# Attention token stages: tail keys of four heads on four 64x64 tiles of TensorE, output halves in two banks

## What is computed

```python
q = _split_heads(query @ Wq.T + bq)
k = _split_heads(key @ Wk.T + bk)
v = _split_heads(value @ Wv.T + bv)
scores = jnp.einsum('bhqd,bhkd->bhqk', q, k)
scores = scores * tau[:, :, None, None] + delta[:, None, None, :]
p_attn = jax.nn.softmax(scores / jnp.sqrt(DK), axis=-1)
x = jnp.einsum('bhqk,bhkd->bhqd', p_attn, v)
x = x.transpose(0, 2, 1, 3).reshape(query.shape[0], -1, H * DK)
return x @ Wo.T + bo
```

## Time and profile before

| | |
|---|---|
| runs | 3376.84 us median of 3 (3376.42 to 3385.39) |
| profiled execution | 3380.68 us, its span 3378.9 us |
| mean granted TensorE clock | 0.978 |
| token stage of layer 0, 12 turns in the middle | 199.4 to 831.4 us |
| token stage of layer 1, 12 turns in the middle | 2040.5 to 2648.1 us |

### The profile page before, as it was taken

One profiled execution on the slowest core, in us unless ns is written; L12 is line 12 of the kernel. 1 busy time (PEld: TensorE's weight loads), 2 busy tenths in 40 slices (PEclk: granted clock), 3 DMA queues, 4 the chain that ended last, 5 costly groups with the idle time before them and its releaser, 6 DMA issues. The chain is left out here.

```text
span 3378.9 us, 55655 instructions
## 1 busy us (share of the span) xinstructions
PE 3197.8 (95%) x17324; PEld 2506.5 (74%) x17324; DVE 2735.5 (81%) x5290; ACT 1560.9 (46%) x5449; POOL 2081.7 (62%) x2335
## 2 busy tenths in 40 slices
PE   7999999999979999999999699999999969999998
PEld 5677777777648888888888577777777757778886
DVE  4788888888677887888887379999999879967775
ACT  1766767667521111111111377777777745321111
POOL 1776666766536777777777477777777753443333
PEclk8999999999979999999999899999999989999999
DMA  7345454454465667676766544555554457730111
GB/s 218 100 137 173 122 166 140 137 174 125 141 174 154 171 169 175 170 166 166 176 164 156 112 128 133 160 163 143 151 172 135 138 164 286 274 103 13 26 13 25
DMA packets 284781, 490.97 MB, mean 145 GB/s; under 512 B 54018, under 2 KB 74818, under 8 KB 283778
## 3 DMA queue, kind: packets, MB, share of 16 engines
q1 hardware_dynamic: 243698, 408.87, 39.6%
q0 software_dynamic: 32256, 77.65, 12.4%
q10 hardware_dynamic: 8592, 1.57, 0.3%
HBM read 250.32 MB, written 136.96 MB: 115 GB/s over the span
## 5 line engine op out<-in xcount | busy, mean ns | idle before, releaser
L915 ACT ACTIVATE c_pr<-ps,t_negmax 128x154 f32<-128x154 f32 x1024 | 385.7, 393 | 180.8 <-DVE t_negmax L684 178.6
L684 DVE TENSOR_REDUCE t_negmax<-ps 128x4 f32<-128x616 f32 x512 | 403.6, 788 | 53.3 <-PE ps L980 52.6
L915 ACT ACTIVATE t_pr<-ps,t_negmax 128x154 f32<-128x154 f32 x1024 | 385.6, 393 | 105.8 <-DVE t_negmax L684 101.4
L707 DVE COPY t_pTm<-ps 128x512 f32<-128x512 f32 x448 | 306.0, 683 | 127.3 <-PE ps L993 123.0
L609 POOL TENSOR_TENSOR t_pr<-t_pr,t_inv 128x512 f32<-128x512 f32 x256 | 275.7, 1077 | 191.0 <-DVE t_inv L699 189.3
L609 POOL TENSOR_TENSOR c_pr<-c_pr,t_inv 128x512 f32<-128x512 f32 x256 | 272.0, 1063 | 196.4 <-DVE t_inv L699 195.0
L980 PE MATMUL ps<-t_kst,t_stack 98*128 98x154 f32 x2048 | 353.0, 291 | 26.3 <-DMA t_stack<-t_q_low 10.1
L980 PEld LDWEIGHTS ps<-t_kst,t_stack 98*128 98x128 f32 x2048 | 279.6, 194 | 38.9 <-issue 17.8
L81 PE MATMUL ps<-e_xT_high,e_wgu_high 128*128 128x512 f32 x768 | 302.4, 394 | 1.4 <-DVE e_xT_low L1508 1.4
L83 PE MATMUL ps<-e_xT_high,e_wgu_low 128*128 128x512 f32 x768 | 299.6, 390 | 0.0
L82 PE MATMUL ps<-e_xT_low,e_wgu_high 128*128 128x512 f32 x768 | 299.4, 390 | 0.0
(11 more groups left out here) (373 smaller groups left out, 9320.9 us busy)
## 6 DMA issues: line engine op xcount, KB each, us to landing
t_stack<-t_q_high SPq DMA_DIRECT2D x1016, 64.0 KB, 2.0
c_wgu_in<-in_gate_upT SPq DMA_DIRECT2D x32, 1536.0 KB, 6.4
t_stack<-t_q_low SPq DMA_DIRECT2D x512, 64.0 KB, 2.0
x_dram<-c_wide_rows SPq DMA_DIRECT2D x32, 1024.0 KB, 7.8
c_wd_in<-in_downT SPq DMA_DIRECT2D x32, 768.0 KB, 4.5
t_xbo<-in_x SPq DMA_DIRECT2D x16, 1024.0 KB, 7.0
xw_dram<-t_z SPq DMA_DIRECT2D x16, 1024.0 KB, 5.3
t_xbo<-x_dram SPq DMA_DIRECT2D x16, 1024.0 KB, 11.0
```

Source lines behind the costliest of these rows:

```text
L684: dve.tensor_reduce(negmax[:, u, :], flat[:, at:at + HG * APART].rearrange("p (h n) -> p h n", h=HG)[:, :, 0:KEYS], AX, ALU.max, negate=Tr ...
L707: dve.tensor_copy(pTm[:, g % 2, :, t * P:(t + 1) * P], ps[:, 4, :].rearrange("p (h n) -> p h n", h=HG)).then_inc(s["pTm"], 1)
L915: op = act.activation(pr[:, u % 4, h, :], flat[:, col:col + KEYS], ACT.Exp, bias=negmax[:, u, h:h + 1], accum_out=total[:, u, h:h + 1])
```

## The change

The tail values of two heads become one block of 52 rows (`PROWS`) and 64 columns, and four such products run on four 64x64 tiles of the array: array rows 0 to 51 and 64 to 115 (`HIGH` is 64), columns 0 to 63 and 64 to 127. Each covers 256 tokens. The result lies in two banks, 5 and 6, the first 256 tokens in one and the rest in the other. For the second two token tiles of a group the heads are kept in swapped pairs (`place`), so that their tails come out of the transpose on the other half of the rows. The main products run as eight matmuls of 256 tokens instead of four of 512. Queries and projections move from bank 6 to bank 7.

The four tail transposes of a group run together in a step of their own (`tail_transposes`, steps `TT`), and `p_transposes` has four transposes instead of five. `tails` has eight slots instead of four, and POOL clears it once at the start of the stage. The transposes use bank 5 too, so they wait until the output of the group before is out of it (`oT_out`). The steps of `V`, `PT`, `OO` and `OL` change. In layer 1, `values` of group 2 go from step 3 to step 1 and those of group 3 from 6 to 7; in layer 0, `V` stays.

```diff
-    for h in range(HG):
-        sp.dma_start(scr[f"vt{l}"].rearrange("b (n h) (g e d) -> h (b n) g e d", h=HG, e=HG, d=DK)[h, :, :, h, :],
-                     k["vt"][:].rearrange("n (g e d) -> n g e d", e=HG, d=DK)[:, :, h, :]).then_inc(s["stored"], 16)
+    for b in range(B):
+        for e in range(2):
+            sp.dma_start(scr[f"vt{l}"][b, e * KTAIL:(e + 1) * KTAIL, :].rearrange("n (q e d) -> n q e d", e=2, d=DK)[:, :, e, :],
+                         k["vt"][b * KTAIL:(b + 1) * KTAIL, :].rearrange("n (q e d) -> n q e d", e=2, d=DK)[:, :, e, :]
+                         ).then_inc(s["stored"], 16)
...
-        V = (15, 24, 2, 7) if gate else (15, 23, 3, 6)
+        V = (15, 24, 2, 7) if gate else (15, 23, 1, 7)
+        TT = (12, 20, 30, 5) if gate else (12, 20, 29, 5)
...
-        OL = (23, 30, 4, 9) if gate else (17, 27, 5, 9)
+        OL = (18, 27, 4, 9) if gate else (17, 26, 3, 9)
...
-        PT = (11, 19, 28, 3) if gate else (11, 19, 27, 4)
-        OO = (16, 26, 2, 7) if gate else (15, 24, 4, 7)
+        PT = (12, 20, 30, 5) if gate else (12, 20, 29, 5)
+        OO = (16, 25, 2, 7) if gate else (15, 24, 2, 7)
...
-            sp.dma_start(vt[:, g * P:(g + 1) * P], scr["vt%d" % l][b, :, g * P:(g + 1) * P]).then_inc(s[f"v_in{g}"], 16)
+            for r in (0, HIGH):
+                sp.dma_start(vt[r:r + PROWS, g * P:(g + 1) * P],
+                             scr["vt%d" % l][b, :, g * P:(g + 1) * P]).then_inc(s[f"v_in{g}"], 16)
...
+            pool.memset(tails[:], 0.0).then_inc(s["ready"], 1)
...
+                if v % TG == 0:
+                    reached(pool, s["tail_mm"], GROUPS * i + v // TG - 1)
...
-                dve.tensor_tensor(oT[1][:, k, :], ps[:, B_BANK, :], oT[0][:, k, :].bitcast(F32),
+                dve.tensor_tensor(halves(oT[1][:, k, :]), ps[:, O_BANKS, 0:HALF], halves(oT[0][:, k, :]).bitcast(F32),
                                   ALU.subtract).then_inc(s["oT_out"], 1)
...
             def p_tail_out(i, g):
-                act.wait_ge(s["p_mm"], UNITS * i + TG * (g + 1))
+                act.wait_ge(s["tail_mm"], GROUPS * i + g + 1)
...
                 for h in range(HG):
-                    pe.transpose(ps[:, 4, h * P:(h + 1) * P], pr[:, v % 4, h, 0:P], ident[:])
-                pe.transpose(ps[0:TROWS, 5, t * P:(t + 1) * P], tails[:, v % 4, :],
-                             ident[:]).then_inc(s["p_mm"], 1)
+                    mm = pe.transpose(ps[:, 4, h * P:(h + 1) * P], pr[:, v % 4, place(h, t), 0:P], ident[:])
+                mm.then_inc(s["p_mm"], 1)
+
+            def tail_transposes(i, g):
+
+                pe.wait_ge(s["normed"], 2 * (UNITS * i + TG * g + TG))
+                reached(pe, s["oT_out"], GROUPS * i + g)
+                for t in range(TG):
+                    at = (HIGH + PROWS) * ((TG * g + t) % 8)
+                    mm = pe.transpose(ps[0:HIGH + PROWS, 5, t * P:(t + 1) * P], tails[:, at:at + HIGH + PROWS], ident[:])
+                mm.then_inc(s["tail_mm"], 1)
...
-                pe.matmul(ps[:, B_BANK, :], vt[:, g * P:(g + 1) * P], pTt[:], start=True, stop=False,
-                          skip_group_check=True)
-                for h in range(HG):
-                    mm = pe.matmul(ps[h * DK:(h + 1) * DK, B_BANK, :], vm[:, g * P + h * DK:g * P + (h + 1) * DK],
-                                   pTm[:, g % 2, h, :], start=False, stop=True, skip_group_check=True)
+                for half in range(2):
+                    for q in range(2):
+                        r = HIGH * (q if half == 0 else 1 - q)
+                        pe.matmul(ps[HIGH * q:HIGH * (q + 1), 5 + half, 0:HALF],
+                                  vt[r:r + PROWS, g * P + HIGH * q:g * P + HIGH * (q + 1)],
+                                  pTt[r:r + PROWS, half * HALF:(half + 1) * HALF], start=True, stop=False,
+                                  skip_group_check=True)
+                for half in range(2):
+                    for h in range(HG):
+                        mm = pe.matmul(ps[h * DK:(h + 1) * DK, 5 + half, 0:HALF],
+                                       vm[:, g * P + h * DK:g * P + (h + 1) * DK],
+                                       pTm[:, g % 2, h, half * HALF:(half + 1) * HALF], start=False, stop=True,
+                                       skip_group_check=True)
                 mm.then_inc(s["pv"], 1)
...
+                    if at in TT[:3] and cur:
+                        tail_transposes(i, TT.index(at))
+                    if at == TT[3] and prev:
+                        tail_transposes(i - 1, GROUPS - 1)
                     if at in V[:2] and cur:
                         values(i, V.index(at), batch)
```

More of the change, by code:

```diff
@@ L28 @@
 GROUPS = HEADS // HG
-TROWS = HG * KTAIL
+PROWS, HIGH = 2 * KTAIL, P // 2
 DC = D // P
@@ L46 @@
 UNITS = TG * GROUPS
+HALF = GTOK // 2
 KROWS = 3 * DK + 2
@@ L214, in key_value_phase @@
         dhigh, dlow = (sb(f"delta_{part}", [P, B, KEYS], F32R) for part in ("high", "low"))
-        zero = sb("zero", [TROWS, D])
+        zero = sb("zero", [PROWS, D])
         ps = c["ps"]
@@ L231, in _ @@
                 sp.dma_start(scr[f"vt{l}"].rearrange("b t d -> t b d"),
-                             zero[:].unsqueeze(1).to_broadcast([TROWS, B, D])).then_inc(s["cleared"], 16)
+                             zero[:].unsqueeze(1).to_broadcast([PROWS, B, D])).then_inc(s["cleared"], 16)
             for half in range(2):
@@ L314, in token_phase @@
         pr = c["pr"] if gate else sb("pr", [P, 4, HG, KEYS])
[L315 to L318, removed]
+        tails = sb("tails", [P, 8 * (HIGH + PROWS) + HIGH - PROWS])
+        pTm, pTt = sb("pTm", [P, 2, HG, D]), sb("pTt", [HIGH + PROWS, D])
+        total, mv = sb("total", [P, UNITS, HG]), sb("mv", [P, 2, TG, 2])
         ve, rstd = sb("ve", [P, 2, TG]), sb("rstd", [P, 2, TG])
@@ L407, in last, with place, halves @@
             return isinstance(j, int) and j == NG - 1
+        def place(h, t):
+            return h if t < TG // 2 else (h + 2) % HG
+        def halves(v):
+            return v.rearrange("p (b n) -> p b n", b=2)
         def o_bank(j, t):
@@ L608, in normalize @@
                 main, tail = pr[:, v % 4, :, 0:P], pr[:, v % 4, :, P:KEYS]
-                pool.tensor_tensor(main, main, inv[:, v, :].unsqueeze(2).to_broadcast([P, HG, P]),
+                pool.tensor_tensor(main, main, total[:, v, :].unsqueeze(2).to_broadcast([P, HG, P]),
                                    ALU.mult).then_inc(s["normed"], 1)
-                pool.tensor_tensor(tails[:, v % 4, :].rearrange("p (n h) -> p h n", h=HG), tail,
-                                   inv[:, v, :].unsqueeze(2).to_broadcast([P, HG, KTAIL]),
-                                   ALU.mult).then_inc(s["normed"], 1)
+                if v % TG == 0:
+                    reached(pool, s["tail_mm"], GROUPS * i + v // TG - 1)
+                at = (HIGH + PROWS) * (v % 8)
+                for_pairs = tails[:, at:at + P].rearrange("p (q m) -> p q m", q=2)[:, :, 0:PROWS]
+                pool.tensor_tensor(for_pairs.rearrange("p q (e n) -> p q e n", e=2),
+                                   tail.rearrange("p (q e) n -> p q e n", q=2),
+                                   total[:, v, :].rearrange("p (q e) -> p q e", q=2).unsqueeze(3)
+                                   .to_broadcast([P, 2, 2, KTAIL]), ALU.mult).then_inc(s["normed"], 1)
             def turn(i, par, prev2, prev, cur, nxt, nxt2, before, batch):
@@ L914, in turn @@
                             col = BASE[u % 2] + h * APART
-                            op = act.activation(pr[:, u % 4, h, :], flat[:, col:col + KEYS], ACT.Exp,
-                                                bias=negmax[:, u, h:h + 1], accum_out=total[:, u, h:h + 1])
+                            to = place(h, u % TG)
+                            op = act.activation(pr[:, u % 4, to, :], flat[:, col:col + KEYS], ACT.Exp,
+                                                bias=negmax[:, u, h:h + 1], accum_out=total[:, u, to:to + 1])
                             if n == 0:
```

23 lines of the change are left out of this document (11 added, 12 removed).

## The result

The changed kernel takes 3400.0 us (median of 4 runs, 3398.18 to 3401.66) against 3379.26 (median of 4, 3376.42 to 3385.39): a ratio of 1.0053, 95% interval 1.004 to 1.0067. It is slower by 0.5%, 20.7 us. In the profiled executions the span went from 3378.9 to 3396.2 us, so there are 17.3 us to find.

| part of the span, us | before | after | change |
|---|---|---|---|
| up to the first `values` of layer 0 | 99.5 | 106.3 | +6.8 |
| 15 turns of layer 0 | 783.2 | 777.5 | -5.7 |
| from there to the first `values` of layer 1 | 1058.5 | 1056.8 | -1.7 |
| 15 turns of layer 1 | 757.0 | 780.3 | +23.3 |
| the rest | 680.7 | 675.3 | -5.4 |

The account below looks back on a forecast made before the run. PE was taken to bound layer 0 and DVE layer 1. Terms -18.6 + 20 - 3 + 1 + 1.5 + 1 + 1 - 1 = +1.9 us gave 3382.6, a 3379 median; forecast range 3370 to 3389, 8 in 10 runs 3348 to 3405.

Parts of the forecast that it names:

- SP's chain: Rival, layer 0: scores waiting for SP's `stack` copies wait longer, up to 0.5 us a turn back, 3387 us; chance 0.07.
- the product that doesn't get shorter: Rival: eight main matmuls with 16 loads take 1.3 us, not 1.02, so `values` stays at 1.95; 3399 us; chance 0.13.
- `values`: PE's product for a group: 1.68 us instead of 1.95, tail 0.64 and main products 1.02, a saving of 0.27.
- The two rivals about the product: Tail tiles not at once (3410 to 3429 us or over 3450, chance 0.09); product not shorter (3399 us, chance 0.13).
- Layer 0, -18.6: Layer 0's turns: -1.24 us each over 15 turns, from shorter `values` and transposes moved into their own steps.
- Layer 1, step 1: DVE stands 1.6 to 1.7 us for unit 14's transposes, now behind group 2's `values`; 0.49 given back later.
- Layer 1, size: Layer 1's turns: +1.35 us each, +20 over 15 turns, less about 3 for vanishing PE waits for `stack`.
- step 29: Layer 1: group 2's tail transposes ahead of unit 15's scores make DVE's maximum and PE's step 1 0.24 us later.
- Layer 1 gains too: Rival: slack in DVE's order hides the step 3 wait, up to 1.1 us a turn gained, 3346 us; chance 0.33.
- Stores, +1.5 and +1: Eight tail-value stores instead of four: +1.5 us in layer 0, where all engines wait, and +1 in layer 1.
- POOL's clearing of `tails`: Clearing 940 elements ahead of the first splits: 0.8 us, twice, 0 to 1.6, taken as +1.
- The rest, -1: First and last turns save `values` time without the DVE wait: -1 us.

Follow-up runs that it names:

- the early `xbo`: Five edits together plus layer 0's `xbo` load issued ahead of the next batch's keys and values in SP's queue, on the changed kernel: 3361.1 us.
- the early query: Layer 0's query 2 two steps earlier (high part step 8, low part step 9): 3391.1 us on the changed kernel, 3378.8 us on the kernel before.
- the block behind unit 15: Layer 1's tail transposes of group 2 at step 30, not 29: changed kernel 3393.8 us; with four other edits, including group 2's old step, 3361.7 us.
- two stores: Changed kernel with paired heads' tail rows interleaved, so two DMAs of 104 rows a layer store them, not eight of 26: 3395.5 us.
- the five edits: Changed kernel with layer 1 group 2 `values` at step 3, early query 2, two stores, only gaps of `tails` cleared, tail block at step 30: 3361.7 us.

## Why the prediction was right and wrong

The forecast was no change, +1.9 us on the profiled execution; it became +17.3. The range for 8 in 10 runs, 3348 to 3405, holds the 3400, near its upper end, but the forecast's own, 3370 to 3389, does not: the median rose by 20.7 us, an outcome (slower by more than 10 us) that I had given 0.23. Of the rivals only SP's chain, which I had put down as no change, had a part in it. That another, the product that doesn't get shorter, stood at 3399 is chance, as the product did get shorter. What failed is the size of two large terms that were to cancel: layer 0 gave 5.7 where 18.6 was forecast, and layer 1 took 23.3 where 17 was. Term by term:

- **`values`**: 1.59 us against 1.68 forecast and 1.95 before. The tail took 0.59 for 0.64, the main products 1.00 for 1.02. The two rivals about the product are out. By the rule of the Trainium skill that I had weighed ("TensorEngine Tiling (Array Packing)", section Gotcha 1: PSUM Pressure), the tail would have taken 1.1 by my estimate; the trace disagrees for tiles that write different partitions of a bank.
- **Layer 0, -18.6**: it gave -5.7, and this is the larger of the two misses. A turn in which nothing is late takes 51.60, which is -0.97 and not -1.24 (-14.5 in all). The product saved more than forecast and the turn less. In such a turn PE's starts give 1.53 us less for the four `values` (forecast 1.08), but 0.29 more for the transposes with the scores behind them (forecast 0.16 less), 0.13 more for its other products, and 0.13 more idle time (0.59 to 0.72). Of the other 8.8 us most lie in SP's queue, the rival that I had given 0.07: its chain of copies held unit 8 back in about half of the turns. Started earlier, it gave back 4.3 us in the 15 turns; the early `xbo` gave 3.4 more, at the borders. Before the change the three border turns took 53.07, 52.55 and 52.57 us, and with the early query 52.5 to 52.6, so that the borders cost next to nothing there. 1.1 is not assigned. I had asked for this chain only where it was late already, and not how much lead it had elsewhere, which was 0.3 to 0.7 us.
- **Layer 1, step 1**: the mechanism was right, and shown twice: DVE's wait is 1.68 (forecast 1.6 to 1.7), PE's new wait for ACT's query 2 is 1.02 (forecast), and the old kernel with the step moved loses 1.64 a turn, the new one gains 1.81 when it is moved back.
- **Layer 1, size**: +1.82 a usual turn against +1.35, 23.3 in 15 turns against 20 - 3 (15 times 1.82 would be 27.3, so that about 4 of the long turns before did vanish, where 3 was forecast). The mis-sized terms are step 29, which cost 0.40 in place of 0.24, two waits of 0.2 and 0.3 (residual for PE, low part of x for ACT), and DVE's own work, 0.5 a turn dearer, that the sum did not have.
- **Layer 1 gains too**: false for the change, true for the product. With group 2 at its old step and the block behind unit 15, a turn takes 50.03 against 50.43 before. DVE has that slack; the change spent it, and more, on one step.
- **Stores, +1.5 and +1**: the part ahead of the first `values` grew by 6.8. I bounded eight stores by 4.4 us, since the elements are the same; they took 7.02, 0.88 each, more than a store before (0.55). I had also read the stores wrongly: each has a quarter of the rows (26 of 104), with twice the pieces in a row, and not half of the rows. Of the 6.8, 4.5 are the later start of the stage. POOL's clearing of `tails` took 0.88 but cost nothing that shows: this part is 99.4 us with two stores and 99.3 when only the gaps are cleared as well. The rest is not assigned; the part takes 99.5 to 101.3 us in the three traces with the old product, and 105.0 to 106.8 in the six with the new one and eight stores. The +1 for layer 1's stores did not come.
- **The rest, -1**: it was -5.4. Of it 4.0 is the end of layer 1, from the last turn's first `values` to PE's last output product (45.0 us before, 41.0 after). No run takes that apart; 1.4 in the stages behind is not assigned.

## What to carry over

Before a step is moved, ask how much lead the engine that does it has over the one that waits for it, at the old place and at the new. Just behind a wait an engine has no lead, so the worst place for new work is there, and turning the order round within the step only changes who waits. When a stage gets shorter, list the chains that run beside it with the lead that each has today: one of them is the next limit, and here SP's queue took about half of the gain in layer 0. With the five edits around it the product was worth having, 0.6% faster than before. Of the five, the old kernel might have gained by two without it: by the early query, which was run there and gave nothing beyond the noise, and by the two stores, which were not run there (its four take 2.18 us in all).

## What the runs showed of the hardware

**Tiles on different array rows in one bank.** Four 64x64 tiles, two of them on other array rows than their neighbour and all on their own partitions of two banks, start within 0.02 us of each other, and their two passes take 0.59 us in all. The Trainium skill, "TensorEngine Tiling (Array Packing)", section Gotcha 1: PSUM Pressure, says that different row tiles can't access one bank at the same time; no sign of that is in this trace.

**A small DVE copy beside POOL.** One DVE copy of 4 columns, between SBUF tiles, took 0.13 us before and 0.65 after. In the second case it starts at 2478.74 while POOL's product runs, and ends with it, at 2479.4. Before, it was through (2463.95) when POOL's product began (2463.97):

```profile
2463.82 0.13 DVE L830 COPY t_z<-t_score 128x4 f32<-128x4 f32 x1
...
2463.97 1.04 POOL L609 TENSOR_TENSOR t_pr<-t_pr,t_inv 128x512 f32<-128x512 f32 x1 [0.28 <-DVE t_inv L699]
```

```profile
2478.32 1.04 POOL L624 TENSOR_TENSOR t_pr<-t_pr,t_total 128x512 f32<-128x512 f32 x1 [0.28 <-DVE t_total L719]
...
2478.74 0.65 DVE L850 COPY t_z<-t_score 128x4 f32<-128x4 f32 x1
```

The Trainium skill, "SBUF — State Buffer", section "Who interferes with whom", says that a copy can take a mode in which it contends with GpSimd for a pair of ports, locked for a whole instruction; the trace agrees. In twelve turns of layer 1 these copies take 7.8 us in the place of 1.6, and DVE's busy time rose by 5.7 with no work added. They take 7.7 too with `values` back at step 3.

**Narrow stores.** A store holds SP's queue for 0.88 us with 26 rows and for 0.45 us with 104 rows, with eight pieces in a row each.
